# Attention and expert layer on one core: weights loaded and split in parts, first scores pulled forward, list clearing in stages, one drain left out

## The reference

```
xn   = layernorm(x)
q,k,v = xn @ Wq, ctx @ Wk, ctx @ Wv          # 256 x 1024 weights
dots = q @ k.T / 8, masked keys and later keys at -max
x    = x + softmax(dots) @ v @ Wo + bo
xn2  = layernorm(x)
e    = argmax(xn2 @ router_w.T + router_b)   # one expert of 32 for each token
x    = x + relu(relu(xn2 @ w1[e] + b1[e]) @ w2[e] + b2[e])
```

## Time and profile before

| | before |
|---|---|
| median of three runs | 1589.38 us |
| profiled execution | 1589.22 us, span 1587.5 us |
| TensorE (PE) busy | 1485.2 us, 94% |
| VectorE (DVE) busy | 1220.9 us, 77% |
| ScalarE (ACT) busy | 990.3 us, 62% |
| GpSimd (POOL) busy | 332.8 us, 21% |
| TensorE's granted clock, mean | 0.978 of full speed |

### The profile page before, as it was taken

The page is one execution under the profiler, slowest core; times in us unless marked ns, Lnnn a source line. Parts: engine busy times, 40 slices in busy tenths (PEclk is TensorE's granted clock), DMA queues, the critical chain, the costliest instruction groups (busy, mean ns, idle before and its releaser), DMA issues. The chain is left out here.

```text
span 1587.5 us, 45429 instructions
## 1 busy us (share of the span) xinstructions
PE 1485.2 (94%) x13988; PEld 1247.9 (79%) x13989; DVE 1220.9 (77%) x5249; ACT 990.3 (62%) x3110; POOL 332.8 (21%) x505
## 2 busy tenths in 40 slices
PE   4979999999999999999999999999999999975885
PEld 3868888888888888888888888888888888864663
DVE  5757888888888888888888888888888888765663
ACT  4756666666666666666666666666666667643663
POOL 1111111111111111111111111111111111112776
PEclk9989999999999999999999999999999999986997
DMA  7760000000000000000000000000000000004661
GB/s 221 194 196 28 21 27 27 21 27 27 21 27 21 27 27 27 27 21 27 27 21 27 24 24 26 23 27 27 27 22 26 27 27 15 14 15 125 207 177 35
DMA packets 69295, 77.69 MB, mean 49 GB/s; under 512 B 10983, under 2 KB 63373, under 8 KB 69265
## 3 DMA queue, kind: packets, MB, share of 16 engines
q1 hardware_dynamic: 61010, 60.17, 13.4%
q0 software_dynamic: 7680, 16.93, 3.1%
q10 hardware_dynamic: 576, 0.23, 0.1%
HBM read 47.61 MB, written 33.88 MB: 51 GB/s over the span
## 5 line engine op out<-in xcount | busy, mean ns | idle before, releaser
L703 ACT ACTIVATE Sm<-Sm,mneg 128x128 f32<-128x128 f32 (+1 forms) x1024 | 456.2, 450 | 372.4 <-DVE mneg L948 371.7
L948 DVE CUSTOM_DVE_ANT_0 Sm<-psS,MK 128x128 f32<-128x128 f32 (+1 forms) x1024 | 304.5, 354 | 109.2 <-PE psS L544 99.0
L544 PE MATMUL psS<-KT,QT 64*128 64x128 f32 (+1 forms) x2048 | 238.6, 352 | 21.2 <-DVE Sm L965 18.5
L577 PE MATMUL psO<-PT,V 128*64 128x256 f32 (+1 forms) x2048 | 224.1, 340 | 1.3 <-ACT PT L694 1.3
L694 ACT ACTIVATE PT<-psT 128x768 f32<-128x768 f32 x256 | 204.3, 798 | 0.0
L703 ACT ACTIVATION_READ_ACCUMULATOR Sm<-Sm,mneg 128x1 f32 x1024 | 197.2, 193 | 0.0
L544 PEld LDWEIGHTS psS<-KT,QT 64*128 64x128 f32 x2048 | 135.3, 188 | 78.5 <-issue 63.1
L965 DVE SCALAR_TENSOR_TENSOR Sm<-Sm,halve,rinv 128x512 f32<-128x512 f32 x256 | 192.5, 752 | 0.0
L419 POOL DMA_INDIRECT lists<-stg,lrow x64 | 67.9, 1061 | 561.7 <-DVE lrow L905 551.9
L577 PEld LDWEIGHTS psO<-PT,V 128*64 128x64 f32 x2048 | 124.9, 137 | 55.9 <-DVE OT_lo L970 1.5
L561 PEld LDWEIGHTS psT<-ident,Sm 64*128 64x128 f32 x3072 | 138.6, 139 | 25.6 <-issue 1.8
(11 more groups left out here) (156 smaller groups left out, 2944.8 us busy)
## 6 DMA issues: line engine op xcount, KB each, us to landing
lists<-pad SPq DMA_DIRECT2D x8, 1560.0 KB, 16.3
XS<-lists SPq DMA_DIRECT2D x48, 260.0 KB, 2.8
x_in<-in_x SPq DMA_DIRECT2D x32, 256.0 KB, 2.7
ctx_in<-in_ctx SPq DMA_DIRECT2D x32, 256.0 KB, 2.7
xr<-in_x SPq DMA_DIRECT2D x32, 256.0 KB, 2.7
W2R<-in_L_ffn_weights SPq DMA_DIRECT2D x1, 2048.0 KB
out<-Y,tok POOLq DMA_INDIRECT x96
W2R<-in_L_xattn_Wq SPq DMA_DIRECT2D x1, 1024.0 KB, 9.5
```

Of the source, the lines that this page charges most:

```text
L544: last = nc.tensor.matmul(psS[:, side, o:o + (it + 1) * P], QT[rows, p, it * P:(it + 1) * P], KT[rows, p, 0:(it + 1) * P], start=True, sto ...
L577: last = nc.tensor.matmul(psO[DH * side:DH * side + DH, t * P:N], V[:, t, DH * h:DH * h + DH], PT[:, blocks, :], start=(t == 0), stop=(t = ...
L703: nc.scalar.activation(v, v, ACT.Exp, bias=mneg[:, p % 2, k:k + 1], scale=-1.0, accum_out=rsum[:, p % 2, k:k + 1]).then_inc(s_exp, 1)
L948: nc.vector.tensor_tensor_reduce(out=Sm[:, p % 4, side, cols], in0=psS[:, side, cols], in1=MK[:, cols], scale=-SCALE, scalar=3e38, op0=ALU ...
```

## The change

1. Wq, Wk and Wv come in parts. Wq and Wk: the first 256 columns, then the other 768. Wv: two halves of 512 columns. The order on SyncE's queue is x, Wq's first part, context, Wk's first part, the rest of Wq, the rest of Wk, Wv's halves. Wo comes after the next x and context.
2. VectorE subtracts the parts of Wq and Wk, GpSimd those of Wv and Wo. Wo is rounded by ScalarE at step 0 of iteration 0 and subtracted by GpSimd at step 1, and the output projection of step 5 waits for it.
3. The scores of pairs 0 and 1 follow directly behind k0. TensorE runs 22 matmuls of the identity before its first real work and 6 behind the transposes of x.
4. The router's weights and the experts' first bias are laid out transposed by the host (a change of layout only), so their transposes on TensorE and copies on VectorE go; these and the other small loads move from ScalarE's queue to SyncE's, behind Wo.
5. GpSimd's constants come ahead of `root1(0)` and `fold(0)` instead of behind.
6. Lists are cleared in three stages: three parts ahead of `step_loads(0)`, three behind `step_loads(1)`, two behind `step_loads(2)`. `W2R` is loaded behind `step_loads(0)`.
7. The first block ends without GpSimd's drain; the rows that the last indirect DMAs read from (`stg`) keep their place.

```
-        block = phase.enter_context(nc.Block())
+        block = phase.enter_context(nc.Block(no_gpsimd_drain=True))
...
             sp.dma_start(x_in[:], xv[0]).then_inc(s_x, 16)
-            sp.dma_start(ctx_in[:], cv[0]).then_inc(s_ctx, 16)
-            for i, (n, W) in enumerate((("q", Wq), ("k", Wk), ("v", Wv), ("o", Wo))):
...
+            for i, part in enumerate(PARTS):
+                if part == "ka":
+                    sp.dma_start(ctx_in[:], cv[0]).then_inc(s_ctx, 16)
+                sp.dma_start(raw(part), SOURCE[part[0]].rearrange("(k p) n -> p k n", p=P)[:, :, PARTS[part]]).then_inc(s_w[i], 16)
+            sp.wait_ge(s_xn, 2)
+            sp.dma_start(x_in[:], xv[1]).then_inc(s_x, 16)
             sp.wait_ge(s_ct, 1)
             sp.dma_start(ctx_in[:], cv[1]).then_inc(s_ctx, 16)
+            sp.dma_start(RAW["o"].rearrange("p (k n) -> p k n", k=PAIRS),
+                         Wo.rearrange("(k p) n -> p k n", p=P)).then_inc(s_w[6], 16)
+            sp.dma_start(rwT[:], router_w.rearrange("(k p) e -> p k e", p=P)).then_inc(s_small, 16)
...
             sp.dma_start(W1R[:], w1.rearrange("e (p c) h -> p e (c h)", c=KD)).then_inc(s_w1r, 16)
...
+            sp.wait_ge(s_pad, 2)
+            for part in range(3):
+                clear(part, s_cleared)
             step_loads(0, False, True, B > 2)
+            sp.wait_ge(s_wo_lo, 1)
...
+            sp.dma_start(W2R[0:HID, :, :], w2.rearrange("e h d -> h e d")).then_inc(s_w2r, 16)
...
+            step_loads(1, True, True, True)
+            for part in range(3, 6):
+                clear(part, s_cleared2)
+            step_loads(2, True, True, True)
+            for part in range(6, 8):
+                clear(part, s_cleared2)
...
# GpSimd, ahead of the loop and in iteration 0
+            root1(0)
+            fold(0)
+            lo_ctx(0)
+            for i, part in enumerate(("va", "vb")):
+                pool.wait_ge(s_wsplit, list(PARTS).index(part) + 1)
+                nc.gpsimd.tensor_tensor(lo(part), raw(part), hi(part), ALU.subtract).then_inc(s_vlo, 1)
...
+                    if p == 1 and isinstance(b, int) and b == 0:
+                        pool.wait_ge(s_wo_hi, 1)
+                        nc.gpsimd.tensor_tensor(flat(Wol), RAW["o"], flat(Woh), ALU.subtract).then_inc(s_wo_lo, 1)
...
# TensorE
+            for _ in range(22):
+                nc.tensor.matmul(psT[:, 0, 0:P], ident[:], ident[:], start=True, stop=True)
...
+                if name == "k0":
+                    score_pair(0, 0, True)
+                    score_pair(0, 1)
+            pe.wait_ge(s_small, 80)
+            pe.wait_ge(s_vlo, 2)
             iteration(0, False, True)
...
# ScalarE
+            hi_part("qa")
             act_read("xt", 0, psR[BANK["xt"]])
             hi_ctx(0)
+            hi_part("ka")
+            hi_part("qb")
+            act_read("q0", 0, psR[BANK["q0"]])
+            hi_part("kb")
+            act_read("k0", 0, psR[BANK["k0"]])
+            hi_part("va")
+            hi_part("vb")
             for p in range(2):
                 for side in range(2):
                     exps(0, p, side)
+                if p == 0:
+                    act_read("q1", 0, psR[BANK["q1"]])
+            act_read("k1", 0, psR[BANK["k1"]])
+            act_read("q2", 0, psR[BANK["q2"]])
...
# VectorE
             halve_of(0)
+            lo_part("qa")
+            dve_read("xt", 0, psR[BANK["xt"]])
+            lo_part("ka")
+            lo_part("qb")
+            for side in range(2):
+                masked(0, 0, side)
+            lo_part("kb")
+            for side in range(2):
+                masked(0, 1, side)
+            stats1(1)
+            apply1(1)
             inverse_sums(0, 0)
             normalise(0, 0)
+            dve_read("v0", 0, psR[BANK["v0"]])
+            dve_read("v1", 0, psR[BANK["v1"]])
```

More of the change, by code:

```diff
@@ L326, in step_loads, with clear @@
                     sp.dma_start(ctx_in[:], batch(cv, b + 2)).then_inc(s_ctx, 16)
-            step_loads(0, False, True, B > 2)
[L330 to L334, removed]
+            def clear(part, done):
+                rows = lists[part * (NROW // 8):(part + 1) * (NROW // 8), :].rearrange("(t p) r -> p t r", p=P)
+                sp.dma_start(rows, pad[:].unsqueeze(1).broadcast_to([P, NET // 8, ROW])).then_inc(done, 16)
+            sp.wait_ge(s_pad, 2)
+            for part in range(3):
+                clear(part, s_cleared)
+            step_loads(0, False, True, B > 2)
+            sp.wait_ge(s_wo_lo, 1)
+            sp.wait_ge(s_vlo, 2)
+            sp.wait_ge(s_wlo, 4)
+            sp.dma_start(W2R[0:HID, :, :], w2.rearrange("e h d -> h e d")).then_inc(s_w2r, 16)
+            sp.dma_start(W2R[HID:HID + 1, :, :], b2.rearrange("e d -> (e d)").unsqueeze(0)).then_inc(s_w2r, 16)
+            step_loads(1, True, True, True)
[4 more added lines that the diff above has]
+                clear(part, s_cleared2)
+            with sp.Fori(3, B - 2) as b:
                 step_loads(b, True, True, True)
@@ L437, in iteration @@
                             if isinstance(b, int) and b == 1:
-                                pool.wait_ge(s_cleared, 128)
+                                pool.wait_ge(s_cleared, 48)
+                            if isinstance(b, int) and b == 3:
+                                pool.wait_ge(s_cleared2, 80)
                             list_rows(b - 1)
@@ L444, in _ @@
             iteration(0, False, True)
-            iteration(1, True, True)
-            with pool.Fori(2, B - 2) as b:
+            for b in range(1, 4):
+                iteration(b, True, True)
+            with pool.Fori(4, B - 2) as b:
                 iteration(b, True, True)
@@ L497, in wo @@
             def wo(part, b):
-                if part == 0 and not (isinstance(b, int) and b == 0):
+                if part == 0 and isinstance(b, int) and b == 0:
+                    pe.wait_ge(s_wo_lo, 1)
+                elif part == 0:
                     pe.wait_ge(s_x1, b)
@@ L624, in _ @@
                 held[BANK[name]] = emptied(name, 0)
-                if name in ("q0", "k0", "v0"):
-                    pe.wait_ge(s_wlo, "qkv".index(name[0]) + 1)
+                if name in need:
+                    pe.wait_ge(*need[name])
                 if name == "xt":
                     xt(0, psR[BANK[name]])
+                    for _ in range(6):
+                        nc.tensor.matmul(psT[:, 0, 0:P], ident[:], ident[:], start=True, stop=True)
                 elif name[0] == "v":
@@ L740, in _, with hi_part @@
             act.dma_start(maskrow[:], mask[0].partition_broadcast(P)).then_inc(s_mask, 16)
[L741 to L745, removed]
+            def hi_part(part):
+                i = list(PARTS).index(part)
+                act.wait_ge(s_w[i], 16)
+                nc.scalar.activation(hi(part), raw(part), ACT.Copy).then_inc(s_wsplit, 1)
+            hi_part("qa")
             act_read("xt", 0, psR[BANK["xt"]])
             hi_ctx(0)
-            for step in ("q", "k", "v", "q0", "k0", "o", "q1", "k1", "q2"):
-                if step in SPLIT:
-                    act.wait_ge(s_w["qkvo".index(step)], 16)
-                    nc.scalar.activation(flat(SPLIT[step][0]), RAW[step], ACT.Copy).then_inc(s_wsplit, 1)
-                else:
-                    act_read(step, 0, psR[BANK[step]])
+            hi_part("ka")
[5 more added lines that the diff above has]
+            hi_part("vb")
             for p in range(2):
@@ L1014, in iteration, with lo_part @@
                         halve_of(b + 1)
+            def lo_part(part):
+                dve.wait_ge(s_wsplit, list(PARTS).index(part) + 1)
+                nc.vector.tensor_tensor(lo(part), raw(part), hi(part), ALU.subtract).then_inc(s_wlo, 1)
             stats1(0)
```

79 lines of the change are left out of this document (27 added, 52 removed).

## The result

The changed kernel takes 1570.03 us (median of four runs; 1569.75 without the longest) against 1589.28 us, 0.9875 of the time, interval 0.9855 to 0.9894: faster by 1.25%, clear of the noise. The forecast was 1566.6, range 1559 to 1576. One run of the changed kernel (1631.46 us, mean clock 0.929) and all runs of the first two groups of experiments, the kernel before included, took some 60 us longer with TensorE at the low level nearly throughout the second block where a trace shows it; so times are compared only as ratios within a group, and stages by the traces.

What follows compares the result with a forecast made beforehand. TensorE bounds the long middle, so the change acts only at the edges. The terms -8.5 - 2.0 + 0.5 + 2.0 - 10.4 - 4.2 = -22.6 take 1589.2 to 1566.6 us, range 1559 to 1576.

Steps and rivals of the forecast that it cites:

- Start: Before iteration 0: its scores start at 30.0 instead of 38.51, a gain of 8.5 us, bounds -1.3 and 15.8.
- low-clock rival: In the new prologue, TensorE stays at the low level: 8.1 us more, 1574.7 us in all; chance 0.16.
- Clock: TensorE comes into iteration 0 at the high level, a gain of 2.0 us, bounds 0 and 2.4.
- Wo: Inside iteration 0: ScalarE's rounding of Wo costs 0.5 us and GpSimd's subtraction of it 2.0 us.
- first term: Iteration 0, step 0: k2's read stands behind ScalarE's rounding of Wo, costing 0.5 us, bounds 0 and 1.9.
- second term: Iteration 0: GpSimd's 5.0 us subtraction of Wo holds VectorE's normalising, costing 2.0 us, at most 5.0.
- Stall: Iteration 1: the wait for a mask row behind eight list clearings goes whole, a gain of 10.4 us, down to 0.
- Drain: Between the blocks: without GpSimd's drain, 4.2 us are gained, bounds 0 and 7.9, reaching the end undiminished.
- rival that the drain gives nothing: Between the blocks: the barrier waits for GpSimd all the same, 1570.8 us in all; chance 0.05.
- likeliest case: Whole kernel: the forecast with every term as taken, 1566.6 us; chance 0.55.
- blocked port's rival: Iteration 0: Wo's 5.0 us block in full (+3.0) and a mask row 3 us past its margin (+3.0), 1572.6; chance 0.12.
- a TensorE gap in iterations 0 to 3: Sign in the first block's iterations 0 to 3: idle TensorE there would make the prediction wrong; no size given.

Runs made afterwards that it cites:

- the filled gap: The changed kernel with 20 identity matmuls on TensorE at the head of step 4 of iteration 0, where it waits for normalising; ratio 0.9867.
- the first experiment: The changed kernel with GpSimd's subtraction of Wo moved ahead of its wait for batch 1's mask row; ratio 0.9844.

## Why the prediction came out

The time lay 3.4 us above the forecast because errors cancelled in part: Wo cost 5.6 us more than priced, the start gave 1.3 more, and 2.4 came by luck. Smaller differences lie in the drain (0.4), among the outputs (0.5) and around the span (1.1). Step by step:

- *Start* (-8.5): -9.84, of which up to 0.6 may be x's earlier landing by chance. Right in mechanism and within 1.3 us in size. No run takes the start's parts one by one, but for the identity matmuls, so how the gain divides is read from the trace. The low-clock rival was mispriced for this kernel: even without the identity matmuls 1.2 to 1.7 us are lost, not 8.1, as the first chunks bring the high level themselves (without them, in the first of the two runs, pairs of matmuls take 0.63 us up to 16.3 and 0.40 from 16.7 on). The granted clock reads 1.00 there all along; the level is taken from the durations, since pairs at 0.50 later in that trace take 0.63 too.
- *Clock* (-2.0): -1.98 in step 0, as forecast.
- *Wo* (+2.5, its two terms +0.5 and +2.0): +1.48 and +6.59, and this is the step that failed. The first term named the right wait, k2's read behind ScalarE's rounding, and was too small; it has slack on the mean of an iteration, but not at that place. The second term failed in the overlap: "I take 2.0, half of it less some slack", with 5.0 as the upper bound. The row of before had shown the rule (the VectorE operation ends 0.3 us behind GpSimd's), but it was averaged over the phase instead of asked: what releases GpSimd's subtraction? The mask row does, at 45.0, and a normalising operation stands at 46.27. The bound also forgot what follows: CT_lo holds the second operation (1.75 us instead of 0.74), and the gap lets the clock fall (some 2 us by the filled gap). Ten traces give one line: in the nine in which normalising began inside the subtraction it ended 0.27 to 0.29 us behind it (4.40, 3.74, 3.73, 3.59, 1.74 and four times 0.71 us long), and in the one in which it began behind it, it took 0.48. The Trainium skill says the same (SBUF — State Buffer, "Who interferes with whom": the shared port pair is an exclusive lock). The runs here agree.
- *Stall* (-10.4): -10.36, and 10.3 when staged alone. The mask row at 45.0 was forecast at 44 (43.4 / 8 is 5.4 us a clearing, not 5.2, which gives 44.3). Its margin, from the landing to the rounding of the context, was forecast at 3.5 and is 47.12 - 45.02 = 2.1.
- *Drain* (-4.2): -4.31 at the second block's first rows, as forecast, but -3.77 at the first output (-3.78 alone), so it does not reach the end "undiminished"; some 0.5 us more is lost again among the outputs. The first load stands 2.52 us behind the last write, as forecast. The rival that the drain gives nothing falls by both runs on it.
- *Not in the sum*: 2.36 us of luck with the clock in the last output projection of the first block. Without it the profiled execution would have stood near 1572.7, by an estimate from this one trace; whether the two unprofiled runs (1568.34 and 1569.75) had the same luck is not known.

So the range held, but the likeliest case did not happen as described: it was the blocked port's rival, larger than priced and without its mask row, offset by a better start and by that luck. By the prediction's own list of signs it was wrong in one: a TensorE gap in iterations 0 to 3. One reading of its first page was off too, without effect: the last five slices are low in the earlier trace rows, not four.

## What to carry to other kernels

Before moving an elementwise operation to GpSimd, ask which event releases it and which VectorE operation with two SBUF inputs stands within its length: the price is the overlap, from nothing to all of it, and it can be set by moving two lines. Price a TensorE gap with the low clock that may follow it (some 2 us behind a gap of 4.7 here, none behind one of 2.0). And when an experiment shifts a later stage against another, read the stages, not the total: two of these totals came out for the wrong reason.

## What was not expected of the hardware

In ten of the fourteen traces TensorE fell to the low level early in the second block and was still there at 1600, although the windows between show it busy all the time; here a stretch of the first experiment:

```profile
1436.00:1440.00 4.00, 2.77 (x14) 2.03 (x15) 2.97 (x10) 2.66 (x7) 2.04 (x3) 0.70 0.46 111
1500.00:1540.00 40.00, 40.00 (x167) 28.39 (x167) 16.48 (x52) 16.32 (x40) 19.45 (x20) 0.50 0.40 125
```

In iteration 0 of the changed kernel it had come back after 56, with TensorE busy 2.00 of 2 us in the windows from 54 on. What tells the two apart stays open, as does what decides the fall in the first block's last output projection, which the same kernel showed in one profile and not in the other.
